# Attention hands on undivided sums and its denominators apart, in a fused attention and FP4 feed-forward kernel

## The reference

```python
def layer(x):                      # x: 8 x 1024 x 512, float32
    n = layernorm(x)
    c_q, c_kv = n @ W_DQ, n @ W_DKV                 # 128 wide
    Q = [c_q @ W_UQ, rope(c_q @ W_QR)]              # 16 heads, 32 + 16 wide
    K = [c_kv @ W_UK, rope(n @ W_KR)];  V = c_kv @ W_UV
    w = softmax(where(causal, clip(Q @ K.T, -80, 80), -inf) / sqrt(48))
    x = x + (w @ V) @ W_O
    h = silu(fp4(n2) @ fp4(w_gate).T) * (fp4(n2) @ fp4(w_up).T)   # n2 = layernorm(x), 1408 wide
    return x + fp4(h) @ fp4(w_down).T               # fp4: blocks of 16, scale = max / 6
```

## Time and profile before

| | |
|---|---|
| median of 3 runs | 3168.64 us (3168.17 to 3169.87) |
| profiled execution, its own time | 3172.8 us |
| its span | 3170.6 us |
| PE busy | 3027.9 us (95%) |
| DVE busy | 2652.8 us (84%) |
| ACT busy | 1272.6 us (40%) |
| POOL busy | 652.1 us (21%) |

### The profile page before, as it was taken

The page is one execution under the profiler, slowest core; times in us unless marked ns, Lnnn a source line. Parts: engine busy times, 40 slices in busy tenths (PEclk is TensorE's granted clock), DMA queues, the critical chain, the costliest instruction groups (busy, mean ns, idle before and its releaser), DMA issues.

```text
span 3170.6 us, 65004 instructions
## 1 busy us (share of the span) xinstructions
PE 3027.9 (95%) x23436; PEld 2215.5 (70%) x23436; DVE 2652.8 (84%) x4432; ACT 1272.6 (40%) x1881; POOL 652.1 (21%) x600
## 2 busy tenths in 40 slices
PE   7999599999999999989999999999999999999999
PEld 6777444444444444457888888888888888888887
DVE  7999478888888888878888888888888888888886
ACT  4455266767666676743222222222222222222221
POOL 2433200000000000002222332333232322222332
PEclk9999799999999999989999999999999999999999
DMA  6888835545454554541000000000000000000000
GB/s 217 280 288 274 236 107 127 134 128 130 126 129 126 125 135 124 133 149 36 31 30 30 30 30 30 30 30 28 25 27 29 30 30 30 30 30 30 30 24 14
DMA packets 209162, 285.30 MB, mean 90 GB/s; under 512 B 16592, under 2 KB 116816, under 8 KB 209104
## 3 DMA queue, kind: packets, MB, share of 16 engines
q1 hardware_dynamic: 209104, 284.52, 30.4%
HBM read 173.05 MB, written 111.41 MB: 90 GB/s over the span
## 4 chain that ended last, share of the span: by engine, by line
PE 55%; DVE 1%; ACT 0%; issue 0%; POOL 0%; DVEq 0%
PE p_ring L1642 19%; PE p_ring L1670 15%; PE ps_od L1642 11%; PE ps_od L1622 5%; PE p_ring L1660 2%; PE p_ring L1650 1%; PE ps_od L1670 0%; PE p_ring L1622 0%; DVE sb_wg_lo L1538 0%; PE p_ring L1685 0%; DVE sb_fp_tmp L102 0%; DVE sb_wd_lo L1538 0%; DVE sb_h_amax L88 0%; DVE sb_stage L1509 0%; PE ps_od L1685 0%
## 5 line engine op out<-in xcount | busy, mean ns | idle before, releaser
L845 ACT ACTIVATE sb_probs<-scores 128x1024 f32<-128x1024 f32 (+3 forms) x768 | 586.1, 813 | 325.8 <-PE scores L1063 321.3
L908 DVE TENSOR_SCALAR sb_probs<-sb_probs 128x2048 f32<-128x2048 f32 (+3 forms) x320 | 288.1, 900 | 66.6 <-ACT sb_probs L845 66.5
L1078 PE MATMUL ps_od<-sb_probs,sb_v 128*32 128x512 f32 (+3 forms) x3072 | 328.2, 499 | 0.0
L1340 POOL TENSOR_TENSOR sb_stage<-sb_stage,sb_h_inv 128x512 f32<-128x512 f32 (+1 forms) x192 | 210.6, 1097 | 543.3 <-DVE sb_h_inv L94 543.3
L1063 PEld LDWEIGHTS scores<-sb_q_hi,sb_k_hi 32*128 32x128 f32 x1536 | 73.9, 182 | 328.2 <-ACT sb_probs L845 286.5
L1642 PE MATMUL p_ring<-sb_wg_hi,sb_xq_hi 128*128 128x512 f32 (+1 forms) x1024 | 295.3, 369 | 0.3 <-DVE sb_wd_lo L1538 0.3
L1642 PE MATMUL p_ring<-sb_wg_lo,sb_xq_hi 128*128 128x512 f32 (+1 forms) x1024 | 290.9, 365 | 0.0
L1642 PE MATMUL p_ring<-sb_wg_hi,sb_xq_lo 128*128 128x512 f32 (+1 forms) x1024 | 289.9, 364 | 0.0
L1670 PE MATMUL p_ring<-sb_wd_hi,sb_ht_hi 128*128 128x512 f32 x693 | 275.9, 398 | 0.0
L1670 PE MATMUL p_ring<-sb_wd_hi,sb_ht_lo 128*128 128x512 f32 x693 | 270.2, 390 | 0.0
L1670 PE MATMUL p_ring<-sb_wd_lo,sb_ht_hi 128*128 128x512 f32 x693 | 269.8, 389 | 0.0
(11 more groups left out here) (194 smaller groups left out, 6692.8 us busy)
## 6 DMA issues: line engine op xcount, KB each, us to landing
kq<-sb_kq_out SPq DMA_DIRECT2D x32, 1024.0 KB, 6.3
sb_kq_raw<-kq SPq DMA_DIRECT2D x64, 512.0 KB, 4.2
sb_xin<-in_L_attn_x_dram SPq DMA_DIRECT2D x32, 512.0 KB, 5.6
rq<-sb_r_out SPq DMA_DIRECT2D x64, 256.0 KB, 2.9
v<-sb_v_out SPq DMA_DIRECT2D x64, 256.0 KB, 3.6
sb_qr<-rq SPq DMA_DIRECT2D x256, 64.0 KB
sb_kr_hi<-kr SPq DMA_DIRECT2D x32, 512.0 KB
sb_kr_lo<-kr SPq DMA_DIRECT2D x32, 512.0 KB
```

The costliest lines, as they stand in the source:

```text
L845: act.activation(probs[:, k % PROBS, 2 * pair:2 * pair + 2, off:BANK], scores[(2 * k + pair) % RING2][:, :, off:BANK], ACT.Exp, scale=SCAL ...
L908: i = dve.tensor_scalar(pr, pr, P_MAX, P_MIN, ALU.min, ALU.max)
L1078: mm = pe.matmul(ps_o[rows, off:BANK], v_sb[s][:, j, rows], probs[:, k % PROBS, i, off:BANK], start=(j == 0), stop=last)
L1340: pool.tensor_tensor(x, x, spread(h_inv[:, a // QB:b // QB], (b - a) // QB), ALU.mult).then_inc(h_y, 1)
```

## The change

- The division is gone from attention. `copy_out`'s result is stored as it is; a new copy on ACT, `copy_denominators`, brings `ps_d` to SBUF after the exponentials of body 5 (half 0) and of body 0 of the next group (half 1), and SP stores one row for each head (`dn`).
- Once in a pair (s = 1) SP loads the 128x64 denominators of the two groups of the pair before, DVE inverts them in body 9 (`invert_chunk`), and SP stores them (`dinv`).
- In the feed-forward part SP loads the inverses of a tile, spread over 32 partitions a head (`load_inverse`, four DMAs), and POOL multiplies (`divide_tile`), once for each tile.
- DVE adds the two sums up once more (`add_sums`, bodies 9 and 10), and PE takes that one total in weigh(11) in place of one sum in weigh(7) and one in weigh(9).
- Small jobs move. On DVE the second half of the query split goes from body 9 to body 4, and the product that starts or ends a weight piece (`w_y`, `w_done`) from body 4 to body 11. On ACT the constant product of the weight piece goes from body 6 to body 11. On SP the stores stand ahead of the loads of the next group, and `load_piece`, `store_piece` go to the end of the body.
- The loads of W_O and of the first tiles no longer stand behind `store_piece` in the last group. There are 7 slots for weight blocks in place of 8, and 32 matmuls of warm-up in place of 20.

```diff
-SUM_LAG = 2
-WARM_UP = 20
+TOTAL_STEP = NS - 1
+WARM_UP = 32
-LATE = {28: 8, 29: 9, 30: 10, 31: 11, 32: 7, 33: 2}
+LATE = {28: 7, 29: 8, 30: 9, 31: 10, 32: 2, 33: 1}
+    def divide_tile(self, pool, i, inverses, loads):
+        pool.wait_ge(self.in_loaded[i], loads)
+        pool.wait_ge(self.inv_loaded, inverses)
+        at = self.at_in[:, i]
+        pool.tensor_tensor(at, at, self.inv_in[:], ALU.mult).then_inc(self.at_divided, 1)
+    def invert_chunk(self, dve):
+        dve.reciprocal(self.chunk[:], self.chunk[:]).then_inc(self.chunk_inverted, 1)
...
             def store(it2, s, half):
-                sp.wait_ge(normed, half_no(it2, s, half) + 1)
+                sp.wait_ge(o_free, half_no(it2, s, half) + 2)
                 sp.dma_start(t["at"][it2 * 2 + s, :, half * BANK:(half + 1) * BANK],
                              o_sb[:, half, :]).then_inc(at_stored[half], 16)
+                sp.wait_ge(d_free, half_no(it2, s, half) + 2)
+                sp.dma_start(dn_v[it2 * 2 + s, :, half * BANK:(half + 1) * BANK],
+                             d_sb[0:P:DH, :]).then_inc(d_stored[half], 16)
...
+            def copy_denominators(it2, s, half):
+                act.wait_ge(pv_done, step_no(it2, s, NS if half else 4) + PROBS)
+                act.wait_ge(d_stored[1 - half], it2 * 32 + (s * 16 + 16 + 16 * half))
+                act.copy(d_sb[:], ps_d).then_inc(d_free, 1)
...
+                    if k == 0 and not first:
+                        copy_denominators(*preceding(it2, s), 1)
+                    if k == 5:
+                        copy_denominators(it2, s, 0)
-                    if k == 6 and s == 0:
+                    if k == 11 and s == 0:
                         act.wait_ge(w_y, it2 + 1)
                         act.mul(w_big[:], w_sb[:], MAGIC).then_inc(w_magic, 1)
...
+            def add_sums(it2, s, pair):
+                own(dve, summed, sums(it2, s, 1) + (pair + 1))
+                heads = slice(2 * pair, 2 * pair + 2)
+                dve.tensor_tensor(added[:, 0, heads], added[:, 0, heads], added[:, 1, heads], ALU.add).then_inc(total, 1)
...
                     elif k == 10:
-                        invert(it2, s, 0)
-                        turn_back(it2, s, 0)
-                    elif k == 11:
-                        normalise(it2, s, 0)
-                        if not last:
-                            turn(it2, s, 1)
+                        add_sums(it2, s, 1)
+                    elif k == 11 and s == 0:
+                        own(dve, w_scaled, scaled + 4)
+                        dve.wait_ge(w_stored, it2 * 16 + 16)
+                        dve.tensor_tensor(w, blocks_of(w_in[:]), spread(w_inv[:], WP // QB), ALU.mult).then_inc(w_y, 1)
...
-                for n, x in enumerate(SUMS):
-                    if k == x[1] + SUM_LAG:
-                        pe.wait_ge(summed, sums(it2, s, n + 1))
-                        sources.append((added[:, n], 0, n == 0))
                 if not any(k in x for x in SUMS):
-                    sources.append((probs[:, k % PROBS], off, j == 0))
+                    sources.append((probs[:, k % PROBS], off, j == 4 * half))
+                if k == TOTAL_STEP:
+                    pe.wait_ge(total, totals(it2, s) + 2)
+                    sources.append((added[:, 0], 0, False))
...
-PREP_SLOTS = 8
+PREP_SLOTS = 7
...
                 if n == 11:
-                    sp.wait_ge(normed, 1)
+                    sp.wait_ge(o_copied, 1)
                     sp.dma_start(t["at"][B * GROUPS - 1, :, BANK:S], last_o[:]).then_inc(last_stored, 16)
+                    sp.wait_ge(d_copied, 1)
+                    sp.dma_start(last_dn, last_d[0:P:DH, :]).then_inc(last_stored, 16)
```

More of the change, by code:

```diff
@@ L780, in body @@
                         load(*following(it2, s))
[L781 to L788, removed]
+                if s == 1 and not (isinstance(it2, int) and it2 == 0):
+                    sp.wait_ge(ahead.chunk_stored, it2 * 16 + 16)
+                    for h in range(HALF):
+                        sp.wait_ge(d_stored[h], it2 * 32 + 16)
+                    ahead.load_chunk(sp, it2 - 1)
                 if not (isinstance(it2, int) and it2 == G2 - 1):
@@ L800, in body @@
                         ahead.load_job(sp, n, ahead.stage[:, n])
+                    sp.wait_ge(ahead.at_divided, 1)
+                    ahead.load_inverse(sp, 0, 1)
                 store(it2, s, 0)
+                if s == 1 and not (isinstance(it2, int) and it2 == 0):
+                    sp.wait_ge(ahead.chunk_inverted, it2)
+                    ahead.store_chunk(sp, it2 - 1)
+                if s == 0:
+                    if not (isinstance(it2, int) and it2 == G2 - 1):
+                        sp.wait_ge(w_y, it2 + 1)
+                        load_piece(it2 + 1)
+                else:
+                    store_piece(it2)
             groups(sp, body)
@@ L1305, in body @@
                     store(b, j - 1)
+                if exists(q, r + 3):
+                    sp.wait_ge(ahead.at_divided, count(q, r, 1, 3))
+                    ahead.load_inverse(sp, b, j + 3)
+                if isinstance(b, int) and (b, j) == (0, 1):
+                    sp.wait_ge(ahead.chunk_inverted, 2 * B)
+                    ahead.store_chunk(sp, 2 * B - 1)
+                if isinstance(b, int) and (b, j) == (0, 2):
+                    sp.wait_ge(ahead.chunk_stored, 16 * (2 * B + 2))
             for j in range(TILES):
@@ L1326, in _, with divide @@
                 pool.sem_inc(stored[i], 16)
+            def divide(q, r):
+                ahead.divide_tile(pool, r % 2, count(q, r, 16 * NI, 16 * NI), count(q, r // 2 * 2, 16, 32))
             def rest_of_attention(q, r):
@@ L1367, in round_attention @@
             def round_attention(q, r):
-                act.wait_ge(in_loaded[r % 2], count(q, r // 2 * 2, 16, 32))
+                act.wait_ge(ahead.at_divided, count(q, r, 1, 1))
                 if exists(q, r - 1):
@@ L1410, in round_job @@
                 act.copy(split_at(n)[0], job_out(n)).then_inc(hi, 1)
+            act.wait_ge(ahead.pv_done, all_weighed)
+            act.copy(last_d[:], ring[3][:, 1]).then_inc(d_copied, 1)
             for n in range(GATE_JOBS):
@@ L1600, in body @@
                     result(q, r - 1)
+                if first:
+                    dve.wait_ge(ahead.chunk_loaded, 16 * 2 * B)
+                    ahead.invert_chunk(dve)
             iterations(dve, body)
```

172 lines of the change are left out of this document (81 added, 91 removed).

## The result

The changed kernel takes 3177.66 us (median of 8 runs, 3175.0 to 3180.58) against 3168.93 us before in the same comparison (8 runs, 3168.17 to 3170.44). The ratio is 1.0025, 95% interval 1.0016 to 1.0034: slower by 8.7 us, where 4.0 us faster was forecast. The profiled execution took 3178.2 us.

A forecast was written before the change was run, and what follows sets the result against it. Attention decides, through PE's own work and the score-exponentials-score chain over ACT; PE is full in the feed-forward part. -53.9 + 11.4 + 38.7 - 1.1 + 0.9 = -4.0 us, giving 3164.6 us; 8-in-10 range 3142 to 3184.

The forecast's parts named there:

- The feed-forward part: POOL's new product, 1.17 us, stretches DVE at most by its length, within 1.54 us slack a tile: no cost.
- The rival that I gave for this part: Feed-forward part: POOL's product reaches PE once a tile's DVE work grows over 1.54 us; 38 us, 3203 us; chance 0.06.
- PE's saving: Attention bodies 8 and 10: one matmul set less in each, 0.87 us apiece, 1.74 a group, 53.9 us in all.
- The boundary s = 1 to s = 0: Between groups: score(1') to score(3') 5.50 us against 4.74, from the total's matmuls and ACT's new copy; 11.4 us more.
- The boundary s = 0 to s = 1: Between groups: ACT's constant product waits for DVE's product behind a clip; 7.16 us against 4.74, 16 times, 38.7 us more.
- Attention's sum: Attention's groups and boundaries together: -53.9 + 11.4 + 38.7 us; a pair of groups about 0.3 us shorter than 61.5.
- The end of attention: Up to the next part: no W_O wait, against late DVE work and a store; 1.1 us earlier, bounds 3 earlier, 4 later.
- DVE becomes what PE waits for: Attention steps 8 and 10: DVE over 0.6 us later loses the second saving, 27 us, 3191 us; chance 0.16.
- a sign of being wrong that the prediction had named: In attention, PE showing waits for clips in steps 9 to 11 would make the forecast wrong; no size given.
- The term of 0.9 us at the start of the feed-forward part: First weight blocks: last store behind one more slot's load, and a second store behind it; 0.9 us later, bounds 0 and 2.

The follow-up runs named there:

- experiment 6: The changed kernel with 48 idle semaphore increments behind DVE's increment of `raw_split`, its feed-forward loop on DVE at instruction 752; 3171.74 us (ratio 1.0003).
- 7: The kernel before with 80 idle semaphore increments behind DVE's increment of `raw_split`, its feed-forward loop at instruction 832; 3169.96 us (ratio 0.9999).
- 8: The changed kernel without the feed-forward loads of inverse denominators from the third tile on, POOL's product kept; 3171.13 us (ratio 1.0002).
- experiment 4: The changed kernel with DVE's product for the weight piece ahead of the clip of step 0' instead of behind it; 3145.85 us (ratio 0.9926).
- Kernel 12: As kernel 5, but with 96 idle increments in place of 48, DVE's feed-forward loop at instruction 800; 3143.09 us.
- experiment 9: As kernel 5, but with the two sums weighed apart again, no additions of sums, and 64 idle increments in place of 48; 3182.52 us (ratio 1.0059).
- 3: The changed kernel without loads of inverse denominators and POOL's product in the feed-forward part from the third tile on; 3171.26 us (ratio 1.0004).
- kernel 5: Experiment 4 plus 48 idle increments behind DVE's increment of `raw_split`, its feed-forward loop at instruction 752; 3143.10 us (ratio 0.9913).
- kernel 11: As kernel 5, but with 64 idle increments in place of 48, DVE's feed-forward loop at instruction 768; 3141.04 us.

## Why the prediction was wrong

**The step that failed** is "The feed-forward part": "DVE waits 92.6 / 60 = 1.54 us a tile for PE, so I take nothing." The slack was there, and the product on POOL (1.35 us in the mean, not 1.17) stayed within it, as experiment 6 shows; where it met DVE it cost DVE 0.5 to 1.1 us, less than its full length. What used it up was not in the sum: a refetch of DVE's loop, which came with its new place, at the moment of the four loads of the inverses. Neither alone costs anything to be measured: refetch without loads 3169.96 us (7), loads and product without refetch 3171.74 (6), refetch and product without loads 3171.13 (8). Together, at this place of the loop, they make a stall of up to 3.5 us, and the part takes 6 to 7 us more (2.8 us with experiment 4's edit). Kernel 12 has both, at another place, and loses nothing. The rival that I gave for this part was right that DVE's slack decides, but had the wrong mechanism, and put the threshold too low: in 8 DVE is up to 2.2 us late, not 1.54, and PE does not wait.

**PE's saving**: right, 0.86 in either body for 0.87, and experiment 9 gives it back. **The boundary s = 1 to s = 0**: right, 5.56 against 5.50. **The boundary s = 0 to s = 1**: right to the hundredth, 7.16, with ACT's wait for `w_y` as its cause; experiment 4 takes the cause away and the cost with it. But the step was incomplete: what PE's clock did behind the wait wasn't in it, 2 x 1.6 = 3.2 us in the profiled execution.

**Attention's sum**: a pair of groups is 61.3 us, before 61.5. From the first group's score(4) to the last group's it is 952.2 us in the profile of 8, which has no dip of the clock, and 954.6 to 954.7 in those of before and 7: 2.4 us less, 3.8 forecast: 0.01 in each of 62 bodies and 0.06 in each of 15 boundaries are missing, which makes 1.5. With two dips it is 955.4.

**The end of attention** was mis-sized: 1.1 us earlier forecast. From the last group's score(4) to POOL's `MEMSET` it is 28.4 us (28.2 and 28.3 in 6 and 8), before 29.1 and in 7, the same kernel but for the padding, 28.1: nothing. In the last group PE waits for DVE, which has additions, an inversion, the products of W_O and the piece's product in its queue:

```profile
1384.79 0.64 PE L1124 MATMUL ps_od<-sb_probs,sb_v 128*32 128x256 f32 x8 [0.84 <-DVE sb_probs L982]
...
1387.52 0.43 PE L1124 MATMUL ps_od<-sb_probs,sb_v 128*32 128x128 f32 x8 [1.67 <-DVE sb_probs L974]
1388.66 0.65 PE L1137 MATMUL ps_od<-sb_probs,sb_ones 128*32 128x128 f32 x8 [0.71 <-DVE sb_added L999]
```

That is 3.2 us of waits, the rival "DVE becomes what PE waits for", in one group of 32; it is a sign of being wrong that the prediction had named (PE showing waits for clips in steps 9 to 11), seen in this group alone. In 9, without the additions, the same stretch is 26.3 us. The term of 0.9 us at the start of the feed-forward part can't be told from the scatter: in 6 that part takes 1777.1 us in all, before 1777.2.

From the forecast, 3164.6, to the time: about 6 us for the stalls, 3 for the clock, 1.4 for attention's sum and 1.1 for its end make 3176; 1.6 us are left, within the scatter of the runs (3175.0 to 3180.6). The 3 for the clock are those of the profiled execution; no other run of the changed kernel has a trace. That the stalls are the larger part is shown by 6. That a dip of the clock follows from PE's wait rests on 8 of 80 against 0 of 144 boundaries; why it follows in 8 and not in the other 72 is open. That the loads make the fetch slow is shown by 3, 8 and the packets' times; by which of the shared resources (the DMA engines, their rings, the memory) is open.

## What to carry to other kernels

Adding the sums up once more, with the division moved out, is worth having, 27 to 28 us, once the small product that ACT waits for stands ahead of a clip: kernel 5 takes 3143.1 us against 3170.2, kernel 11 3141.0 against 3169.2. Moving the division out does not pay by itself (experiment 9); whether the additions would pay with the division still in attention was not run. A wait that you cost at a boundary costs more than its length where PE idles behind it, since the clock may fall; so ask first which instruction ahead of the waited-for one can go behind it.

When an engine idles with no releaser at the head of a hardware loop, look at the instruction queue's packets before you look at the code around it. A few idle instructions ahead of the loop, in a wait that no transfer depends on, tell whether its place matters, and can be the cure; and don't compare two kernels by a few tenths of a per cent without a look at that count in both, and, where it differs, at the wait at the loop's head: the count alone says nothing of the price (experiments 7 and 12).

## What the runs showed of the hardware

- A loop of 320 DVE instructions is fetched again in every turn or never, by where it stands: 704, 800 and 832 (it reaches into four packets of 128 instructions) against 720, 752 and 768 (three). Five packets of 8 KB a turn.
- The stall at the head of the refetched loop is 0.8 to 1.1 us without the four loads (share of the DMA engines 0.13 in one of them) and 1.35 to 3.53 us with them (0.69).
- After such a fetch DVE's next instruction starts 1.1 to 1.6 us behind the end of the packet (52 turns of four kernels).
- An increment of a semaphore costs DVE about 0.09 us: 48 of them delayed the loads behind them by 4.0 us, 80 by 7.4.
- DVE's product for `sb_xq`, 0.69 us otherwise, took 1.5 to 1.8 us 13 times in experiment 6 and 9 times in the changed kernel, at the time of POOL's product; in 3, without that product, it never took over 0.70.
- After an idle stretch of 1.9 us PE ran at 1.2 GHz for some 3 us in 8 cases of 80, and at 2.4 GHz in the other 72; after one of 3.15 us (experiment 9) and one of 1.97 us in the feed-forward part it ran at 1.2 GHz.
